# Moving q and k of one pair, o's last transpose, and two weight checks in a macaron block on one core

## The reference

```python
x = x + 0.5 * ffn(layernorm(x))       # silu(W1 x) * (W2 x), two ternary 512x512 layers with gelu, W3
x = x + attention(layernorm(x))       # 16 heads of 8, 256 keys, softmax(q k^T / sqrt(8)) v, Wo
x = x + 0.5 * ffn(layernorm(x))
```

## Time and profile before

| | us |
|---|---|
| median of 3 runs | 605.0 |
| lowest and highest | 604.67, 606.29 |
| profiled execution | 609.87 |
| its span | 608.0 |
| TensorE busy | 582.7 |
| ScalarE busy | 466.5 |
| VectorE busy | 446.5 |
| GpSimd busy | 98.4 |

### The profile page before, as it was taken

One profiled execution on the slowest core, in us unless ns is written; L12 is line 12 of the kernel. 1 busy time (PEld: TensorE's weight loads), 2 busy tenths in 40 slices (PEclk: granted clock), 3 DMA queues, 4 the chain that ended last, 5 costly groups with the idle time before them and its releaser, 6 DMA issues.

```text
span 608.0 us, 12581 instructions
## 1 busy us (share of the span) xinstructions
PE 582.7 (96%) x4452; PEld 428.0 (70%) x4452; DVE 446.5 (73%) x1003; ACT 466.5 (77%) x793; POOL 98.4 (16%) x262
## 2 busy tenths in 40 slices
PE   1999999999999999999999999999899999999996
PEld 1878878788786755665656565666678788788784
DVE  6896756858747887988989897886765855955642
ACT  4677877977976667888888888877877977968963
POOL 2074020022013104041322312102020020020000
PEclk9999999999999989999999999999999999999999
DMA  8300000000054505252726353400000001010011
GB/s 277 96 1 1 1 1 1 1 0 0 2 198 167 189 2 191 89 199 81 258 75 226 113 167 140 140 2 1 2 1 0 1 1 36 0 34 0 1 34 37
DMA packets 36693, 42.02 MB, mean 69 GB/s; under 512 B 2464, under 2 KB 27296, under 8 KB 36640
## 3 DMA queue, kind: packets, MB, share of 16 engines
q1 hardware_dynamic: 36640, 41.31, 20.2%
HBM read 22.42 MB, written 18.87 MB: 68 GB/s over the span
## 4 chain that ended last, share of the span: by engine, by line
PE 77%; ACT 9%; DVE 6%; issue 5%; DMA 1%; SPq 1%; ACTq 0%; POOL 0%; DVEq 0%
PE bank L1118 39%; PE bank L1231 11%; PE bank L1205 8%; PE bank L1218 4%; PE bank L1220 3%; ACT silu L546 2%; DVE act_lo L843 2%; DVE silu L852 2%; ACT act_hi L538 2%; PE bank L1187 2%; PE bank L1263 2%; PE bank L1191 2%; PE bank L1249 1%; ACT act_hi L563 1%; PE bank L1195 1%
## 5 line engine op out<-in xcount | busy, mean ns | idle before, releaser
L1118 PE MATMUL bank<-act_hi,WH 128*128 128x512 f32 x576 | 230.3, 400 | 2.3 <-DVE silu L852 1.1
L1118 PE MATMUL bank<-act_lo,WH 128*128 128x512 f32 x576 | 225.7, 392 | 0.0
L893 DVE TENSOR_REDUCE neg_max<-bank 128x2 f32<-128x512 f32 x256 | 167.2, 681 | 24.4 <-PE bank L1205 22.3
L683 ACT ACTIVATE probs<-bank 128x512 f32<-128x512 f32 x256 | 140.8, 596 | 32.7 <-PE bank L1220 30.4
L863 DVE TENSOR_TENSOR act_lo<-full,act_hi 128x512 fp32r<-128x512 f32 x128 | 91.4, 719 | 99.2 <-ACT act_hi L563 98.9
L561 ACT ACTIVATE full<-bank,SG 128x512 f32<-128x512 f32 x128 | 88.2, 689 | 65.7 <-PE bank L1118 64.9
L1118 PEld LDWEIGHTS bank<-act_hi,WH 128*128 128x128 f32 x576 | 108.2, 188 | 29.4 <-ACT act_hi L563 3.5
L1118 PEld LDWEIGHTS bank<-act_lo,WH 128*128 128x128 f32 x576 | 108.3, 188 | 23.3 <-issue 1.0
L1218 PE MATMUL bank<-QK 32*128 32x256 f32 x512 | 87.5, 329 | 0.3 <-ACT probs L683 0.3
L563 ACT ACTIVATE act_hi<-bank,SG 128x512 fp32r<-128x512 f32 x128 | 87.3, 682 | 0.0
L1220 PE MATMUL bank<-m_parts,SEL 32*128 32x256 f32 x512 | 73.7, 276 | 0.0
(11 more groups left out here) (96 smaller groups left out, 570.8 us busy)
## 6 DMA issues: line engine op xcount, KB each, us to landing
qk_scratch<-qk SPq DMA_DIRECT2D x64, 256.0 KB, 2.5
QK<-qk_scratch SPq DMA_DIRECT2D x16, 1024.0 KB, 7.1
raw_rest<-w_ffn SPq DMA_DIRECT2D x4, 512.0 KB, 7.1
out<-X SPq DMA_DIRECT2D x4, 512.0 KB, 3.2
X<-x SPq DMA_DIRECT2D x3, 512.0 KB, 7.2
raw<-w_ffn SPq DMA_DIRECT2D x3, 256.0 KB, 4.9
X<-x SPq DMA_DIRECT2D x2, 256.0 KB, 3.0
WA<-w_att SPq DMA_DIRECT2D x1, 256.0 KB, 4.5
```

What stands on the lines that cost most here:

```text
L683: A.activation(probs[:, v % 8, :], bank[B_BANKS[bb][v]][:, :], ACT.Exp, scale=SCALE)\
L893: D.tensor_reduce(neg_max[:, bb, qt, n0:n0 + 2], bank[(banks or A_BANKS[bb])[u]][:, :].rearrange("p (h k) -> p h k", h=2), axis=AX.X, op=A ...
L1118: ins = MM(dst, a, b, start=k == 0, stop=k == len(todo) - 1)
```

## The change

Three things are changed.

- In the second slot of the attention, `project_q` and `project_k` of pair 2 stand at u = 5 and 7 instead of 9 and 11. ScalarE's `full_part` and `high_part` follow at 5, 7 and 6, 8. The other slots keep their order.
- The low halves of weight groups 5 and 6 are no longer reduced by VectorE. ScalarE copies them as unsigned 16-bit numbers into the scratch tile `full`, in tiles 0 and 3 of the first `layer1`, and its accumulator output writes their sum into the two columns of `low_max`. `all_low_bits` waits for these sums as well.
- In the entry of the second feed-forward part, `transpose_o` follows tile 5 instead of 4, `project_out` tile 7 instead of 6, and ScalarE's `o_to_sbuf` tile 5 instead of 4.

```diff
@@ ScalarE @@
+            def low_bits(k):
+
+                act.wait_ge(w_in[k], 16)
+                halves = raw_of(k).bitcast(U16).rearrange("p k (c t) -> p k c t", t=2)
+                A.activation(full[:, 0:2, :], halves[:, :, :, 0], ACT.Copy, accum_out=low_max[:, k:k + 1])\
+                    .then_inc(bits_summed, 1)
+
@@
-                    layer1(t1, {1: lambda: split_x(nb + 1, 1), 2: lambda: weight_hi(6)})
+                    layer1(t1, {0: lambda: low_bits(5), 1: lambda: split_x(nb + 1, 1), 2: lambda: weight_hi(6),
+                                3: lambda: low_bits(6)})
                     act.wait_ge(s3_half, 1)
                 else:
-                    layer1(t1, {0: lambda: evacuate_o(NBATCH - 1), 4: lambda: o_to_sbuf(NBATCH - 1)}, ACT.Gelu)
+                    layer1(t1, {0: lambda: evacuate_o(NBATCH - 1), 5: lambda: o_to_sbuf(NBATCH - 1)}, ACT.Gelu)
@@
-                    if u in (9, 11) and ahead is not None:
-                        full_part(ahead, (u - 9) // 2)
-                    if u in (10, 12) and ahead is not None:
-                        high_part(ahead, (u - 10) // 2)
+                    q_at = 5 if second else 9
+                    if u in (q_at, q_at + 2) and ahead is not None:
+                        full_part(ahead, (u - q_at) // 2)
+                    if u in (q_at + 1, q_at + 3) and ahead is not None:
+                        high_part(ahead, (u - q_at - 1) // 2)
@@ VectorE @@
             def all_low_bits():
+                dve.wait_ge(bits_summed, 2)
                 G = len(W_GROUPS)
-                dve.wait_ge(bits_reduced, G)
+                dve.wait_ge(bits_reduced, G - 2)
@@
-                    layer1(t1, {0: lambda: low_bits(4), 1: lambda: low_x(nb + 1, 1), 2: lambda: low_bits(5),
-                                3: lambda: low_bits(6), 4: all_low_bits, 6: take_flag})
+                    layer1(t1, {0: lambda: low_bits(4), 1: lambda: low_x(nb + 1, 1), 4: all_low_bits, 6: take_flag})
@@ TensorE @@
-                    layer1(t1, nb, general, {2: tokens, 4: lambda: transpose_o(b), 6: lambda: project_out(b)},
+                    layer1(t1, nb, general, {2: tokens, 5: lambda: transpose_o(b), 7: lambda: project_out(b)},
                            range(2, L1_TILES))
@@
-                pe.wait_ge(bits_reduced, len(W_GROUPS) + 1)
+                pe.wait_ge(bits_reduced, len(W_GROUPS) - 1)
@@
-                    if u == 9 and ahead is not None:
+                    if u == (5 if second else 9) and ahead is not None:
                         pe.wait_ge(m_lo, b + 1)
                         project_q(ahead, 6)
-                    if u == 11 and ahead is not None:
+                    if u == (7 if second else 11) and ahead is not None:
                         pe.wait_ge(q_full, ahead)
                         project_k(ahead, 6)
```

More of the change, by code:

```diff
@@ L25 @@
 I16 = mybir.dt.int16
+U16 = mybir.dt.uint16
 I32 = mybir.dt.int32
@@ L172, in macaron_kernel @@
         flag_sum = sem("flag_sum")
+        bits_summed = sem("bits_summed")
         flag_set = sem("flag_set")
```

## The result

| | before | after |
|---|---|---|
| median of 20 runs, us | 607.46 | 604.75 |
| lowest and highest, us | 604.21, 610.61 | 603.43, 605.77 |
| profiled execution, us | 609.87 | 604.83 |
| its span, us | 608.0 | 602.9 |

The ratio of the runs is 0.9955, with a 95% interval of 0.9939 to 0.9972: 2.7 us faster, where 3.9 were forecast. The three runs that the forecast started from had a median of 605.0; 17 more on other occasions lifted it to 607.46. So the changed kernel landed at 604.75, not at 601.1; against the 605.0 that the forecast started from, that is 0.25 us. The spread is as telling as the median: 6.4 us before, 2.3 us after. The chain of the profile keeps its shape: TensorE 76% of it, 77% before.

The account below looks back on a forecast made before the run. The prediction took TensorE, 77% of the chain, to bound the kernel. Its terms, 3.1 + 0.3 + 0 + 0.5 = 3.9 us, taken off the timed median of 605.0, gave 601.1 us, range 600.0 to 605.0.

Parts of the forecast that it names:

- Term a: Second attention slot: q and k earlier keep TensorE's clock at 2.4 GHz; 3.1 us gained, bounds 0 to 3.1.
- R1: Rival, chance 0.25: timed runs before had no low-clock stretch, so only place and later entry pay, 0.8 us; 604.2 us.
- R2: Rival, chance 0.17: second slot's clock still falls at the same time though q and k stand earlier; 603.8 us.
- Term b: Second attention slot: the new place of q and k beside VectorE's work gains 0.3 us, range -0.6 to +0.85.
- part 3: Entry of the second feed-forward part: o's transpose and projection one tile later gain 0.5 us, range 0 to 0.9.
- VectorE is late next: Second attention slot: after the change VectorE sets the end, with the scaled o at about 232.2 us.
- Part 2: First layer1: low halves of weight groups 5 and 6 on ScalarE give 0 us, between 0.05 gained and 0.2 lost.
- R3: Rival, chance 0.08: timed runs before at full clock, then the clock falls behind k in steps 8 to 11; 607.3 us.
- The cause I named for the fall: Second attention slot: six score steps, 3.34 us without a matmul over 128 rows, bring TensorE's clock down.

Follow-up runs that it names:

- the move alone: The kernel before with only q and k of the second slot moved to steps 5 and 7; median 605.19 us, ratio 0.996.
- 32-row fills: The kernel before plus extra 32-row matmuls, results unused, in the second slot; medians 606.43 us with ten, 605.77 with eighteen, 605.94 with twenty.
- the 128-row fill: The kernel before plus two extra 128-row projections of q, results unused, at steps 5 and 7 of the second slot; median 606.84 us.

## Why the prediction was right and where it failed

- **The step that failed is the last one: 605.0 - 3.9.** Term a, 3.1 us, was read from the profiled execution and taken off the median of three runs, none of which, by its time, had the fall: at 604.67, 605.0 and 606.29 they lie with the executions that kept the clock (medians 605.16 to 605.78), not with the fallen ones (medians 609.2 to 610.2, none under 607.9). Their own clocks are not recorded. For those three, R1 was the right case, and it gave 604.2; 604.75 was measured. I saw the gap of 4.9 us between profile and median and named it as the weak point, but gave R1 only 0.25. I argued that the stretch "did not come and go among them", which was true of the three and false of the kernel.
- **Term a is not one number for the kernel.** The fall comes in 43 of 115 executions of the kernel before and in none of 44 of the three kernels with q and k at 5 and 7. When it comes it costs 3.16 us in the trace of the slot (3.1 forecast). So the median fell by 2.7 of the 3.9 us; on chip 6, with 18 of 35 fallen, the move alone took 3.4 us off it. How much of term a a median shows hangs on how many of its executions fell: that the size came out near the forecast is luck. So is it that 604.75 lies inside the range: its upper part, 603.2 to 604.9, came from R1 and R2.
- **Term b, 0.3 us:** 0.35 (13.83 to 13.48), but not by its parts. Starving was 1.15 us behind q and k, where 0.6 was the worst I allowed; the seed was 0.54 us shorter, as expected. The two alone would be a loss. I had left out that the old order at full clock starves VectorE as well, 0.77 us behind k, so that its idle time grew by only 0.26 us in the slot. The size was right in part by luck.
- **The bounds did not follow from the terms:** with b at -0.6 and part 3 at 0, R1 gives 605.6, not 604.9, and the forecast 602.5, not 602.4.
- **VectorE is late next, scaled o near 232.2:** from GpSimd's maxima the slot was forecast at 13.6 us and took 13.48; the chain there runs over VectorE from 224.28 on.
- **Part 2, 0 us:** right. The added instruction took 1.05 + 0.19 us, taken as 1.2; VectorE waited 0.74 us for the silu of tile 4, and TensorE did not.
- **The rule of the Trainium skill on VectorE or ScalarE ("ScalarE: Activation LUTs", Rules for kernel authors), which gives additions and maxima to VectorE:** 1.24 us on ScalarE against 1.21 on VectorE; with both hidden, neither order of preference shows in the time.
- **Part 3, 0.5 us:** the term is 0.69; it was under-sized by 0.19. The wait of 0.9 us before the transpose came out exactly. silu 7 ran 0.69 us earlier, not 0.5: behind the copy of onT, silu 6 followed after 0.26 us and silu 7 after another 1.09, where I had spaced them by 0.4 and 1.15.
- **R2, the fall stays:** it doesn't, 0 of 44. The Trainium skill's page behind it ("TensorE: Matmul & The Clock Gate", last table) ties drops to idle gaps of TensorE between bursts of matmuls. The trace has none ahead of the fall; if the rule is stretched to the small gaps that VectorE's pace leaves inside time booked as busy, it is nearer to the runs than my own cause was, but those gaps are not in the trace.
- **R3, slower through a new fall behind k:** did not happen with both moved, though 2.2 us of scores follow k (223.82 to 226.00). With q alone moved the clock fell in the steps between q and k, not behind k, and the median was 0.5 us above the kernel before on that chip, which is within the noise.
- **The cause I named for the fall,** six steps without a 128-row matmul, was wrong: 32-row fills kept the long falls away, and q alone, with its 128 rows, did not. The cure itself is shown (0 of 44). That it worked because the two projections take the place of gaps is the reading that is left, not shown by itself.

**What stays open:** why a given execution of the same program falls and another doesn't. The start of the work varies by 2.7 us between executions; that it decides was not tried. Nor is it shown what exactly is counted: the fills say that more work in the gaps means fewer falls, no more than that. The fallen executions of the kernel before lie 3.7 to 4.5 us above the others, while the slot accounts for 3.16; the rest may be the later start that the profiled one had (0.96 us), or a second fall in the entry, which cost 1.61 us in the profile of the 128-row fill. The later entry, with its wait of 0.90 us, showed no fall in four profiles, the old one two in ten; what that part does for the clock was not tested by itself.

## What to carry to other kernels

When a profiled execution is several us off the timed ones, find the stretch that makes it so before a term read there is taken off their median, and weigh the term by how often it occurs. A matmul engine that is paced by another looks busy in the profile and may still lose its clock: count matmuls per us against an unpaced stretch, and put work that must be done anyway into the gaps, both pieces of it. A few hidden matmuls can serve where there is none to move: here eighteen or twenty left no long fall in 23 executions, though three short ones, and cost a part of what they saved.

## What the runs showed of the hardware

- TensorE's clock fell from 2.4 to 1.2 GHz for 6.8 us in the profiled execution, with TensorE booked as busy for 3.34 of the 3.34 us before it; by their mean clock, 43 of 115 executions of that program fell. The mean clock per execution, about 0.993 against 0.998, sorts most of them: the medians of the two groups differ by 3.7 to 4.5 us, though one execution at 0.997 took 608.84 us.
- The extra work that came with fewer falls can be nearly free: eighteen 32-row matmuls (2 us) made the slot 0.3 us longer (14.13 against 13.84), where two 128-row projections of the same length made it 1.1 longer (14.93).
- Behind a wait of 1.82 us in the entry of the second feed-forward part the clock also fell in two of the ten profiled executions that have this wait; in one of them it was at 0.54 for 3.55 us.
- VectorE's seed, an operation on 128x4 numbers, took 0.16 us by itself and 0.71, 0.70 and 0.41 us where it began beside GpSimd's subtraction; each time it ended within 0.03 us of the subtraction's end (234.45 and 234.42 us in the kernel before).
- A ScalarE copy of 16-bit numbers at a stride of two took the same 1.05 us as one of float32, and reading the accumulator 0.19 us more.
